# Group statistics, maxima and bias of a linear-attention block: fp32 matmuls of TensorE moved to VectorE or to one-pass matmuls

## The chip, the cores and the metric

One core of one Trainium2 chip. The metric is the device time of one execution of the program in microseconds; 1215.1 us is the median of three runs of the kernel before (1214.41 to 1216.41).

## The reference

x is 16 images of 64x64 positions with 256 channels, float32. Cut to what is computed:

```
g = group_norm(x)                       # 32 groups of 8 channels, over all positions
q, k, v = split(g @ W_qkv)              # 4096 positions x 256 each
k = softmax(k over the 4096 positions)  # per channel
context = k^T @ v                       # 256 x 256
y = x + (q @ context) @ W_out + b_out
```

The normalization is a scale and a shift per channel, so it can be folded into the matrices: the keys come from x times (scaled W_k), and q, context, W_out, the scale and the skip connection fold into one matrix M per image, so that y = x @ M + bias. The bias of an image is b_out plus what the shift by the mean contributes.

## The kernel before, in words

An image is cut into 8 chunks of 512 positions, a chunk into 4 tiles of 128. x is loaded in two layouts: xt (channels on the partitions, for keys and output) and x_raw (positions on the partitions, for the gather). fp32 precision comes from splitting every operand into a high part (type fp32r, which TensorE takes in one pass) and a low part (the rest), and from adding three one-pass products: high x high, high x low, low x high. ScalarE makes most high parts (xt_hi L676, x_hi L681, e_hi L693), GpSimd the low parts of x (xt_lo L341, x_lo L347), VectorE those of the exponentials (e_lo L924). A matmul whose operands are plain fp32 stands in the trace as two instructions.

Per image b there are three stages on TensorE, interleaved with those of the neighbours:

1. Keys (L399): for each chunk 24 matmuls into ps_k, two chunks in flight. ScalarE copies them to e_raw (L685); VectorE keeps a running maximum mx over the positions (L892). The softmax works with two blocks of 4 chunks (HALF = 4), each with its own maximum per channel.
2. After a block's 4 chunks: turn_max (L447) transposes mx by two TensorE transposes, VectorE reduces along the free axis (block_max, L901), spread_max (L455) brings the maximum back as a row on all 128 partitions by fp32 matmuls against the identity, into PSUM, and VectorE's shift subtracts it from e_raw (L917). ScalarE then takes the exponentials.
3. Gather (L480 to L492): exponentials times x, 24 matmuls a chunk, block 0 into ps_g0, block 1 into ps_e. alpha scales the two blocks to one maximum (block_scales, L906 and L909, then ScalarE's scales, L703). Then combine_u and combine_m make M; take_m ends them on VectorE (L982 to L993).
4. Output (L564, L573): per chunk of 512 positions two halves h of 128 output channels, six matmuls of 512 columns each, into ps_e. ScalarE adds the bias on its way to o_stage (L733), SP stores. The halves wait for o_ready of the same half one chunk earlier.

The chunks of the output are issued in the order 3, 4, 5, 6, 7, 0, 1, 2, with the keys of the next image between them. Block 0's turn_max and spread_max of the next image stand around its chunk 4; block 1's stand inside the gather.

The statistics of image b+1: VectorE's bn_half and bn_sum make per-channel mean and variance; stats_mean and stats_var (L462, L466) average them over groups of 8 channels by an fp32 matmul with the matrix grp; mean_of and var_of finish them on VectorE, rstd_of on GpSimd (L357). bias_sum (L542) multiplies the full-precision M with the negative mean: four fp32 matmuls with one moving column each, placed inside the first output chunk; bias_of (L1001) adds b_mean.

The order of the work on each engine is written out by hand: `images` calls `period` for each image on each engine, and each engine works through its list in order, with semaphore waits. GpSimd in `period`: xt_low(n,0), rstd_of(n), x_low(b,4..7), xt_low(n,1), xt_low(n,2), x_low(n,0..3), xt_low(n,3..7), where n = b+1. SP issues every DMA in order too: the loads of xt for the next image wait for e_ps, the stores for o_ready, the loads of xs (for the statistics of image b+2) for bn_done. The last three output halves of image 14 are kept back and issued in the last image's stages (`late`).

Of the kernel before, what the change touches and what calls it, by code (L numbers as in the profile page):

```python
# [28 lines left out]
POOL_LOW = 3  # L29


def build(nc: bass.Bass, xt: bass.AP, xn: bass.AP, w: bass.AP, b_out: bass.AP, out: bass.AP):
# [11 lines left out]
    with ExitStack() as ctx:  # L44
# [43 lines left out]
        b_col = sb("b_col", [P, CB])  # L88
# [5 lines left out]
        grp = sb("grp", [P, P])  # L94
# [31 lines left out]
        b_mean = sb("b_mean", [P, CB])  # L126
# [18 lines left out]
        filled = sem("filled")  # L145
        consts_ready = sem("consts_ready")
# [88 lines left out]
        def _(sp):  # L235
# [83 lines left out]
        def _(pool):  # L319
            nc.gpsimd.memset(one_col[:], 1.0).then_inc(consts_ready, 1)  # L320
# [51 lines left out]
            def period(b, parity, more, more2):  # L372
                n, np_ = b + 1, 1 - parity
                if more:
                    xt_low(n, np_, 0)
                    if b:
                        rstd_of(n, np_)
# [4 lines left out]
                if more:  # L382
# [7 lines left out]
                    for j in range(3, NCH):  # L390
                        xt_low(n, np_, j)
# [5 lines left out]
        def _(pe):  # L397
# [44 lines left out]
            def turn_max(b, blk):  # L442

                to = max_psum(b, blk)
                pe.wait_ge(max_done, b * (TILES * NCH) + TILES * HALF * (blk + 1))
                for d in range(CB):
                    last = nc.tensor.transpose(to[:, 0, d * P:(d + 1) * P], mx[:, d * P:(d + 1) * P], ident)  # L447
                last.then_inc(t_ps, 1)

            def spread_max(b, blk):  # L450

                to = max_psum(b, blk)
                pe.wait_ge(m_blk_ready, b * 2 + (blk + 1))
                for d in range(CB):
                    last = nc.tensor.matmul(to[:, 1, d * P:(d + 1) * P],  # L455
                                            m_blk[:, blk, d:d + 1].broadcast_to([P, P]), ident,
                                            start=(d == 0), stop=True, skip_group_check=True)
                last.then_inc(bc_ps, 1)

            def stats_mean(b):  # L460
                pe.wait_ge(mv_ready, b + 1)
                nc.tensor.matmul(stats_psum(b, 0), grp[:], mv[:, :, 0], start=True, stop=True).then_inc(mean_ps, 1)  # L462

            def stats_var(b):
                pe.wait_ge(var2_ready, b + 1)
                nc.tensor.matmul(stats_psum(b, 1), grp[:], var2[:], start=True, stop=True).then_inc(var_ps, 1)  # L466
# [71 lines left out]
            def bias_sum(b, parity):  # L538
                pe.wait_ge(m_full_ready, b + 1)
# [298 lines left out]
        def _(dve):  # L838
# [312 lines left out]
```

## Time and profile before

| | us |
|---|---|
| median of 3 runs | 1215.1 |
| profiled execution | 1214.93 |
| its span | 1213.2 |
| TensorE busy | 1190.1 |
| VectorE busy | 842.1 |
| ScalarE busy | 840.1 |
| GpSimd busy | 622.4 |

Granted TensorE clock: 1.00 of full speed over the span (2.4 GHz), in every one of the 40 slices. DMA moves 266.71 MB, 220 GB/s in the mean. Times in the profile are microseconds from the span's start. A busy time counts overlapping instructions of an engine once.

### The profile page before, as it was taken

The page shows a single profiled execution, that of the slowest core. Times are in us where ns is not written, and L with a number is a line of the kernel's source. Part 1 is how long each engine was busy: PE and PEld are TensorE (multiplying, and loading weights), DVE is VectorE, ACT ScalarE, POOL GpSimd, SP SyncE. Part 2 cuts the span into 40 slices and gives each one's busy share as a digit, 9 for nine tenths or more (in the row PEclk, how much of TensorE's full clock was granted, in tenths as well). Part 3 has the DMA queues.
Part 4 walks back from the last instruction along what each step waited for, and adds up shares of the span by engine and source line. Part 5 has one row for each costly group of instructions (what it writes and reads, how often), then busy time and mean ns, then how long its engine had stood idle before and what let it go on. Part 6 is the DMA issues. An engine that isn't in the chain of part 4 may idle for free.

```text
span 1213.2 us, 21447 instructions
## 1 busy us (share of the span) xinstructions
PE 1190.1 (98%) x8460; PEld 1115.8 (92%) x8460; DVE 842.1 (69%) x1582; ACT 840.1 (69%) x1140; POOL 622.4 (51%) x288
## 2 busy tenths in 40 slices
PE   4999999999999999999999999999999999999998
PEld 4998999999899998999989999899999989999897
DVE  6877667676776767768776677766767676676551
ACT  5767768677685776757677686776857768577664
POOL 8664564635645355563655636356463564536520
PEclk9999999999999999999999999999999999999999
DMA  9448666576765758666486665867657576573524
GB/s 339 146 167 294 218 235 205 195 269 208 274 203 199 264 172 294 226 206 237 162 301 229 221 227 183 286 209 252 204 201 263 193 278 225 201 252 122 191 74 170
DMA packets 107077, 266.71 MB, mean 220 GB/s; under 512 B 10208, under 2 KB 10208, under 8 KB 106976
## 3 DMA queue, kind: packets, MB, share of 16 engines
q1 hardware_dynamic: 106976, 265.33, 63.5%
q8 instruction: 67, 1.10, 0.4%
q14 instruction: 34, 0.28, 0.1%
HBM read 198.18 MB, written 67.11 MB: 219 GB/s over the span
## 4 chain that ended last, share of the span: by engine, by line
PE 93%; DVE 2%; ACT 1%; POOL 1%; DMA 1%; issue 1%; SPq 0%; DVEq 0%; POOLq 0%; ACTq 0%
PE ps_k L399 29%; PE ps_e L564 19%; PE ps_e L573 10%; PE ps_g L492 5%; PE ps_e L480 5%; PE ps_e L492 5%; PE ps_e L482 5%; PE ps_g L480 4%; PE ps_g L482 4%; PE ps_g L511 1%; PE ps_g L528 1%; PE ps_g L542 1%; PE ps_g L534 1%; POOL x_lo L347 1%; DVE mx L892 1%
## 5 line engine op out<-in xcount | busy, mean ns | idle before, releaser
L341 POOL TENSOR_TENSOR xt_lo<-xt_raw,xt_hi 128x1024 fp32r<-128x1024 f32 x128 | 307.4, 2404 | 434.5 <-ACT xt_hi L676 309.1
L347 POOL TENSOR_TENSOR x_lo<-x_raw,x_hi 128x1024 fp32r<-128x1024 f32 x128 | 281.4, 2216 | 65.6 <-ACT x_hi L681 56.2
L892 DVE TENSOR_TENSOR mx<-ps_k,mx 128x256 f32<-128x256 f32 x480 | 203.3, 424 | 95.8 <-ACT e_raw L685 74.3
L733 ACT ACTIVATE o_stage<-ps_e,bias 128x512 f32<-128x512 f32 x253 | 170.9, 689 | 114.1 <-PE ps_e L573 114.1
L399 PE MATMUL ps_k<-wk_hi,xt_hi 128*128 128x256 f32 x1024 | 207.1, 284 | 1.0 <-DVE mx L892 0.7
L399 PE MATMUL ps_k<-wk_lo,xt_hi 128*128 128x256 f32 x1024 | 205.5, 283 | 0.0
L685 ACT ACTIVATE e_raw<-ps_k 128x512 f32<-128x512 f32 x256 | 141.4, 596 | 87.2 <-PE ps_k L399 87.2
L849 DVE BATCH_NORM_STATS2 bn<-xs 128x6 f32<-128x512 f32 x240 | 154.5, 686 | 40.7 <-DMA xs<-in_xt_dram 39.5
L693 ACT ACTIVATE e_hi<-e_raw 128x1024 fp32r<-128x1024 f32 x128 | 135.1, 1055 | 60.9 <-DVE e_raw L917 33.0
L399 PEld LDWEIGHTS ps_k<-wk_hi,xt_hi 128*128 128x128 f32 x1024 | 163.4, 190 | 8.7 <-issue 1.8
L399 PE MATMUL ps_k<-wk_hi,xt_lo 128*128 128x256 f32 x1024 | 158.2, 283 | 0.0
L399 PEld LDWEIGHTS ps_k<-wk_lo,xt_hi 128*128 128x128 f32 x1024 | 157.4, 189 | 0.0
L564 PE MATMUL ps_e<-xt_hi,acc_hi 128*128 128x512 f32 x474 | 150.3, 398 | 0.0
L573 PE MATMUL ps_e<-xt_hi,u_lo 128*128 128x512 f32 x474 | 150.2, 398 | 0.0
L564 PE MATMUL ps_e<-xt_lo,acc_hi 128*128 128x512 f32 x474 | 148.8, 395 | 0.0
L681 ACT ACTIVATE x_hi<-x_raw 128x1024 fp32r<-128x1024 f32 x128 | 134.5, 1050 | 11.4 <-DMA x_raw<-in_xn_dram 11.2
L676 ACT ACTIVATE xt_hi<-xt_raw 128x1024 fp32r<-128x1024 f32 x128 | 135.0, 1055 | 3.8 <-DMA xt_raw<-in_xt_dram 3.8
L399 PEld LDWEIGHTS ps_k<-wk_hi,xt_lo 128*128 128x128 f32 x1024 | 137.3, 189 | 0.0
L480 PE MATMUL ps_e<-x_hi,e_hi 128*128 128x258 f32 x512 | 125.8, 283 | 0.7 <-POOL x_lo L347 0.7
L482 PE MATMUL ps_e<-x_lo,e_hi 128*128 128x256 f32 x512 | 125.5, 282 | 0.0
L482 PE MATMUL ps_g<-x_lo,e_hi 128*128 128x256 f32 x512 | 124.8, 281 | 0.0
L480 PE MATMUL ps_g<-x_hi,e_hi 128*128 128x258 f32 x512 | 124.8, 282 | 0.0
(129 smaller groups left out, 1992.7 us busy)
## 6 DMA issues: line engine op xcount, KB each, us to landing
xt_raw<-in_xt_dram SPq DMA_DIRECT2D x128, 512.0 KB, 4.3
x_raw<-in_xn_dram SPq DMA_DIRECT2D x128, 512.0 KB, 3.5
out_dram<-o_stage SPq DMA_DIRECT2D x127, 512.0 KB, 4.5
xs<-in_xt_dram SPq DMA_DIRECT2D x240, 256.0 KB, 5.1
w_setup<-in_w_dram SPq DMA_DIRECT2D x2, 256.0 KB, 10.1
out_dram<-o_stage SPq DMA_DIRECT2D x2, 256.0 KB, 2.0
wk<-in_w_dram SPq DMA_DIRECT2D x1, 256.0 KB, 9.9
wq_t<-in_w_dram SPq DMA_DIRECT2D x1, 256.0 KB, 10.9
```

The lines of the kernel that those rows point to most:

```text
L341: nc.gpsimd.tensor_tensor(xt_lo[:, s], xt_raw[:, s], xt_hi[:, s].bitcast(F32), ALU.subtract).then_inc(xt_lo_ready, 1)
L347: nc.gpsimd.tensor_tensor(x_lo[:, s], x_raw[:, s], x_hi[:, s, :, 0:C].bitcast(F32), ALU.subtract).then_inc(x_lo_ready, 1)
L399: return nc.tensor.matmul(ps_k[:, j % 2, t // 2, (t % 2) * C:(t % 2 + 1) * C], (xt_hi, xt_lo)[xs_][:, slot(j, parity), c, t * P:(t + 1) * ...
L480: nc.tensor.matmul(ps_g[j // HALF][:, d, 0:C + 2], w_, x_hi[:, j % X_SLOTS, t, :], start=(j % HALF == 0 and t == 0), stop=False, skip_grou ...
L482: nc.tensor.matmul(ps_g[j // HALF][:, d, 0:C], w_, x_lo[:, j % X_SLOTS, t, :], start=False, stop=False, skip_group_check=True)
L564: nc.tensor.matmul(out_psum(b, u, h), hi[:, c, h * P:(h + 1) * P], x_[:, s, c, :], start=(n == 0 and c == 0), stop=False, skip_group_check ...
L573: last = nc.tensor.matmul(out_psum(b, u, h), lo[:, c, h * P:(h + 1) * P], xt_hi[:, s, c, :], start=False, stop=(c == CB - 1), skip_group_c ...
L685: nc.scalar.activation(e_raw[:, j, 2 * h:2 * h + 2, :].rearrange("p t c -> p (t c)"), ps_k[:, j % 2, h, :], ACT.Copy).then_inc(k_out, 1)
L693: nc.scalar.activation(e_hi[:, j % E_SLOTS], e_raw[:, j], ACT.Exp).then_inc(e_hi_ready, 1)
L733: nc.scalar.activation(o_stage[:, u % O_SLOTS, h, :], src, ACT.Identity, bias=bias[:, h:h + 1]).then_inc(o_ready, 1)
L849: nc.vector.bn_stats(bn[:, q % CB, q // CB, :], xs[:, q % S_SLOTS, :]).then_inc(bn_done, 1)
L892: nc.vector.tensor_tensor(mx[:], tile, mx[:], ALU.max).then_inc(max_done, 1)
```

## The change

Four things are changed.

- Maxima: turn_max is gone. block_max on VectorE transposes mx in 32x32 squares, reduces each square's rows (quad), moves the results of the partition quarters 1 to 3 to quarter 0 (`move`, a reduce over one element) and reduces again. m_blk, m_all, dm and alpha_q are now 32 partitions by 8. block_diag splits the maxima into high and low part on partitions 0 to 31 and 32 to 63 and multiplies them with stacked 32x32 identities into diag (in u_hi's second half). spread_max is one fp32r matmul of 256 columns: a one-column weight of ones, spread to 128, times diag. spread_scales moves alpha_q back to 128 partitions in 4 moves.
- Statistics: for images 1 to 15 the inputs of the group sums are split into high and low parts (mean_parts, var_parts) and summed in one fp32r matmul of 4 columns; VectorE adds the two results.
- Bias: bias_sum is gone. VectorE multiplies u's product in ps_g0, which take_m reads too, with mean times rstd (scale_mean, b_terms), transposes, reduces, moves, adds b_out and moves back to two columns.
- Output: the second chunk goes to ps_g0, and its halves wait for b_terms_ready; the third waits for the outputs of the first. The first chunk is issued high(h0), high(h1), low(h0), low(h1).

GpSimd gets waits: on var_parts_ready (images after the first) and diag_ready ahead of xt_low(n, 0), and on diag_ready of block 0 ahead of xt_low(n, 5). ScalarE makes grp_r, one_r and eyes at the start. In the first image, block 1's spread_max stands one chunk later in the gather. b_out is loaded as 32x8.

The core of the diff:

```diff
-            def turn_max(b, blk):
-                to = max_psum(b, blk)
-                pe.wait_ge(max_done, b * (TILES * NCH) + TILES * HALF * (blk + 1))
-                for d in range(CB):
-                    last = nc.tensor.transpose(to[:, 0, d * P:(d + 1) * P], mx[:, d * P:(d + 1) * P], ident)
-                last.then_inc(t_ps, 1)
             def spread_max(b, blk):
-                pe.wait_ge(m_blk_ready, b * 2 + (blk + 1))
-                for d in range(CB):
-                    last = nc.tensor.matmul(to[:, 1, d * P:(d + 1) * P],
-                                            m_blk[:, blk, d:d + 1].broadcast_to([P, P]), ident, ...)
+                pe.wait_ge(diag_ready, b * 2 + (blk + 1))
+                nc.tensor.matmul(max_psum(b, blk)[:, 1, 0:C], one_r[:].broadcast_to([P, P]), diag,
+                                 start=True, stop=True).then_inc(bc_ps, 1)
...
+            return (ps_g0 if u == 1 else ps_e)[:, h, :]          # out_psum
...
-                elif u > 0:
-                    pe.wait_ge(o_ready, b * (CB * NCH) + (CB * (u - 1) + h + 1))
+                elif u > 1:
+                    pe.wait_ge(o_ready, b * (CB * NCH) + (CB * (u - 2 if u == 2 else u - 1) + h + 1))
+                elif u == 1:
+                    pe.wait_ge(b_terms_ready, b + 1)
...
                 emit_high(b, parity, 0, 0)
-                bias_sum(b, parity)
+                emit_high(b, parity, 0, 1)
                 emit_low(b, parity, 0, 0)
-                emit_high(b, parity, 0, 1)
                 emit_low(b, parity, 0, 1)
...
             def block_max(b, blk):
+                nc.vector.transpose(turned[:], mx[:]).then_inc(turned_ready, 1)
+                nc.vector.tensor_reduce(quad[:, :, 0], turned[:].rearrange("p (q k) -> p q k", k=Q), AX_X, ...)
+                for r in range(1, QUADS):
+                    last = move(quad[0:Q, :, r], quad[r * Q:(r + 1) * Q, :, 0])
+                nc.vector.tensor_reduce(m_blk[:, blk, :], quad[0:Q], AX_X, ALU.max).then_inc(m_blk_ready, 1)
+            def block_diag(b, blk):
+                move(m_parts[0:Q, :], m_blk[:, blk, :]).then_inc(m_part_hi_ready, 1)
+                nc.vector.tensor_tensor(m_parts[Q:2 * Q, :], m_blk[:, blk, :], m_parts[0:Q, :].bitcast(F32), ...)
+                nc.vector.tensor_tensor(diag..., eyes[:]..., m_parts[:]..., ALU.mult).then_inc(diag_ready, 1)
...
             def bias_of(b):
+                nc.vector.tensor_scalar(b_terms[:, 0, :], ps_g0[:, 0, 0:C], scaled_mean[:, 0:1], None, ALU.mult)
+                nc.vector.scalar_tensor_tensor(out=b_terms[:, 0, :], in0=ps_g0[:, 1, 0:C],
+                                               scalar=scaled_mean[:, 1:2], in1=b_terms[:, 0, :], ...)
+                nc.vector.transpose(b_terms[:, 1, :], b_terms[:, 0, :])
+                nc.vector.tensor_reduce(b_quad[:, 0, :], ...)
+                for r in range(1, QUADS):
+                    last = move(b_quad[0:Q, r, :], b_quad[r * Q:(r + 1) * Q, 0, :])
+                nc.vector.tensor_reduce(b_all[:], ...)
+                for r in range(QUADS):
+                    last = move(bias[r * Q:(r + 1) * Q, :], by_quad[:, :, r])
...
             def period(b, parity, more, more2):              # GpSimd
+                if more and b:
+                    pool.wait_ge(var_parts_ready, n)
+                pool.wait_ge(diag_ready, b * 2 + 2)
                 if more:
                     xt_low(n, np_, 0)
```

VectorE's order: block_max is followed by block_diag everywhere; after block 1's pair come mean_of, block_scales and shift(4), and spread_scales stands ahead of take_first; scale_mean stands ahead of take_u.

## Rows read from the trace of the kernel before

**Rows 1.** Busy us of each engine, its share of the span, its instructions (page).
```profile
PE 1190.1 (98%) x8460; PEld 1115.8 (92%) x8460; DVE 842.1 (69%) x1582; ACT 840.1 (69%) x1140; POOL 622.4 (51%) x288
```
**Rows 2.** Waits of TensorE: who waits for whom, total us, times, longest us.
```profile
PE ps_k L462 <- DVE mv L855: 15.3, 1, 15.3
PE ps_k L447 <- DVE mx L892: 1.9, 2, 1.6
...
PE ps_e L480 <- POOL x_lo L347: 0.7, 2, 0.4
```
**Rows 3.** TensorE's timeline around bias_sum (start, us, what), and that line's instructions.
```profile
675.07 0.95 PE L542 MATMUL ps_g<-neg_mean,acc 128*128 128x1 f32 x8
...
676.43 0.63 PE L564 MATMUL ps_e<-xt_hi,acc_hi 128*128 128x512 f32 x2
676.90 0.63 PE L564 MATMUL ps_e<-xt_lo,acc_hi 128*128 128x512 f32 x2
...
L542 PE MATMUL ps_g<-neg_mean,acc x128: 164/250/250, 82.9 to 1188.2; 128*128 128x1 f32 x128
```
**Rows 4.** TensorE's timeline around block 0's turn_max and spread_max.
```profile
618.06 0.38 PE L447 MATMUL ps_g<-zero_eye,mx 128*128 128x128 f32 x2
...
618.74 0.40 PE L399 MATMUL ps_k<-wk_hi,xt_hi 128*128 128x256 f32 x2
...
621.12 0.61 PE L455 MATMUL ps_g<-zero_eye,m_blk 128*128 128x128 f32 x4
...
622.03 0.63 PE L564 MATMUL ps_e<-xt_lo,acc_hi 128*128 128x512 f32 x2
```
**Rows 5.** TensorE's timeline in the gather stage.
```profile
643.32 0.38 PE L447 MATMUL ps_k<-zero_eye,mx 128*128 128x128 f32 x2
...
644.72 0.28 PE L480 MATMUL ps_g<-x_hi,e_hi 128*128 128x258 f32 x1
...
646.62 0.60 PE L455 MATMUL ps_k<-zero_eye,m_blk 128*128 128x128 f32 x4
...
648.25 0.28 PE L480 MATMUL ps_g<-x_hi,e_hi 128*128 128x258 f32 x1
...
650.15 1.12 PE L492 MATMUL ps_g<-x_hi,e_lo 128*128 128x258 f32 x8
651.11 0.28 PE L480 MATMUL ps_g<-x_hi,e_hi 128*128 128x258 f32 x1
...
653.98 0.28 PE L480 MATMUL ps_e<-x_hi,e_hi 128*128 128x258 f32 x1
```
**Rows 6.** VectorE's timeline: the running maximum of chunk 3.
```profile
615.60 1.87 DVE L892 TENSOR_TENSOR mx<-ps_k,mx 128x256 f32<-128x256 f32 x4 [2.66 <-ACT e_raw L685]
```
**Rows 7.** VectorE's timeline in the gather stage and at take_m's end.
```profile
640.81 1.22 DVE L924 TENSOR_TENSOR e_lo<-e_raw,e_hi 128x1024 fp32r<-128x1024 f32 x1
...
644.71 0.14 DVE L906 TENSOR_REDUCE m_all<-m_blk 128x2 f32<-128x4 f32 x1
644.89 0.83 DVE L909 TENSOR_TENSOR dm<-m_blk,m_all 128x4 f32<-128x4 f32 x1
...
647.26 1.22 DVE L917 TENSOR_TENSOR e_raw<-e_raw,ps_k 128x1024 f32<-128x1024 f32 x1 [1.47 <-PE ps_k L455]
...
674.44 0.80 DVE L993 TENSOR_TENSOR u_lo<-acc,acc_hi 128x512 fp32r<-128x512 f32 x1
```
**Rows 8.** GpSimd's timeline: low parts, numbers as before.
```profile
617.08 2.40 POOL L341 TENSOR_TENSOR xt_lo<-xt_raw,xt_hi 128x1024 fp32r<-128x1024 f32 x1 [3.20 <-ACT xt_hi L676]
...
643.32 2.39 POOL L341 TENSOR_TENSOR xt_lo<-xt_raw,xt_hi 128x1024 fp32r<-128x1024 f32 x1 [7.96 <-ACT xt_hi L676]
...
650.20 2.20 POOL L347 TENSOR_TENSOR x_lo<-x_raw,x_hi 128x1024 fp32r<-128x1024 f32 x1
...
685.42 2.39 POOL L341 TENSOR_TENSOR xt_lo<-xt_raw,xt_hi 128x1024 fp32r<-128x1024 f32 x1 [1.41 <-ACT xt_hi L676]
```
**Rows 9.** TensorE's timeline: low-part keys of chunk 3.
```profile
688.22 1.13 PE L399 MATMUL ps_k<-wk_hi,xt_lo 128*128 128x256 f32 x8
```

More of the change, by code:

```diff
@@ L29 @@
 POOL_LOW = 3
+Q = 32
+QUADS = P // Q
 def build(nc: bass.Bass, xt: bass.AP, xn: bass.AP, w: bass.AP, b_out: bass.AP, out: bass.AP):
@@ L93, in build @@
         eye = [zero_eye[:, P:3 * P], zero_eye[:, 0:2 * P]]
-        grp = sb("grp", [P, P])
+        with nc.sbuf_tensor("grp", [P, P], F32) as grp:
+            pass
+        grp_r = sb("grp_r", [P, P], F32R)
+        one_r = sb("one_r", [P, 1], F32R)
+        var_sum = sb("var_sum", [P, CB])
+        var_parts = sb("var_parts", [P, 2, CB], F32R)
+        mean_parts = sb("mean_parts", [P, 2, CB], F32R)
+        mean_rest = sb("mean_rest", [P, CB])
         mx = sb("mx", [P, C])
@@ L107, in build @@
         u_lo = sb("u_lo", [P, CB, C], F32R)
+        with nc.sbuf_tensor("turned", [P, C], F32) as turned:
+            pass
+        with nc.sbuf_tensor("b_terms", [P, CB, C], F32) as b_terms:
+            pass
         u_hi = sb("u_hi", [P, CB, C], F32R)
+        diag = u_hi[:, 1, :]
         m_lo = u_lo
@@ new lines, in stats_mean @@
+            def stats_mean(b):
+                if b == 0:
+                    pe.wait_ge(mv_ready, 1)
+                    nc.tensor.matmul(stats_psum(b, 0), grp_r[:].bitcast(F32), mv[:, :, 0], start=True,
+                                     stop=True).then_inc(mean_ps, 1)
+                else:
+                    pe.wait_ge(max_done, b * (TILES * NCH))
+                    pe.wait_ge(mean_parts_ready, b)
+                    nc.tensor.matmul(stats_psum(b, 0), grp_r[:], mean_parts[:].rearrange("p k c -> p (k c)"), start=True,
+                                     stop=True).then_inc(mean_ps, 1)
@@ new lines, in stats_var @@
+            def stats_var(b):
+                if b == 0:
+                    pe.wait_ge(var2_ready, 1)
+                    nc.tensor.matmul(stats_psum(b, 1), grp_r[:].bitcast(F32), var2[:], start=True,
+                                     stop=True).then_inc(var_ps, 1)
+                else:
+                    pe.wait_ge(var_parts_ready, b)
+                    nc.tensor.matmul(stats_psum(b, 1), grp_r[:], var_parts[:].rearrange("p k c -> p (k c)"), start=True,
+                                     stop=True).then_inc(var_ps, 1)
@@ L536, in combine_m @@
                     last.then_inc(m_ps, 1)
-            def bias_sum(b, parity):
-                pe.wait_ge(m_full_ready, b + 1)
-                for h in range(CB):
-                    for c in range(CB):
-                        last = nc.tensor.matmul(ps_g0[:, 0, h:h + 1], m_full[:, c, h * P:(h + 1) * P],
-                                                neg_mean[:, parity, c:c + 1], start=(h == 0 and c == 0),
-                                                stop=(c == CB - 1), skip_group_check=True)
-                last.then_inc(bias_ps, 1)
-            def out_psum(b, u, h):
-                if late(b, u, h):
-                    return (ps_k[:, 1, 0, :], ps_k[:, 1, 1, :], ps_k[:, 0, 0, :])[LATE.index((u, h))]
-                return ps_e[:, h, :]
             def emit_high(b, parity, u, h):
@@ L619, in period @@
                 gather_high(b, 0)
-                turn_max(b, 1)
                 if more and b:
@@ L627, in period @@
                     stats_var(n)
-                gather_low(b, 1)
-                for j in range(2, NCH):
+                gather_low(b, 2 if b == 0 else 1)
+                for j in range(3 if b == 0 else 2, NCH):
                     gather(b, j)
```

208 lines of the change are left out of this document (159 added, 49 removed).

## The prediction

> **What bounds the kernel now.** I read the busy shares first, then the waits of each engine, then the timeline of one image from the middle (about 612 to 690 us), because an average can't say which wait ends last. TensorE is busy for 1190.1 of 1213.2 us, VectorE for 842.1 [rows 1]. Of the 23 us that TensorE isn't busy, 15.3 stand before its first matmul; after that its waits are short: 1.9 us for VectorE's running maximum, 0.7 us for GpSimd's low parts of x [rows 2]. So TensorE's own stream is the bound: a microsecond taken out of it is a microsecond of the kernel, as long as nobody else becomes late. The cost of a matmul is not its "mean ns", since matmuls overlap, but the distance between starts: 0.47 us for two of 512 columns (676.43 to 676.90) [rows 3], 0.96 us for eight of about 256 (650.15 to 651.11), so 0.12 each [rows 5].
>
> **What leaves TensorE's stream.** Each price is the distance over the odd instructions, less the ordinary pace of those between.
> - bias_sum: 675.07 to 676.43 is 1.36 us with one ordinary pair of 0.47 [rows 3]: 0.89 us for its eight instructions (an fp32 matmul stands as two; 128 of them, 16 images, by the row that counts them there). 16 x 0.89 = 14.2 us.
> - turn_max: 618.06 to 618.74 is 0.68 us and holds four ordinary matmuls of 256 columns, 0.48 [rows 4]: 0.20 us, twice per image, 32 times, 6.4 us.
> - spread_max as it was: 621.12 to 622.03 is 0.91 us with one pair of 0.47 [rows 4]: 0.44 us, 32 times, 14.1 us.
> - The statistics' matmuls, each in front of eight low-part matmuls of 0.96 us: 643.32 to 644.72 is 1.40, so turn and mean cost 0.44 and the mean 0.24; 646.62 to 648.25 is 1.63, so spread and variance cost 0.67 and the variance 0.23 [rows 5]. 15 images: 7.0 us.
> Together 41.7 us.
>
> **What comes in.** One spread of 256 columns in the one-pass type per block. No row has it in its place; ordinary matmuls of that width and type pace at 0.12 us [rows 5], and half the old spread would be 0.22. I take 0.14, near the ordinary one: 32 x 0.14 = 4.5 us. Each statistic becomes one matmul of four columns for two instructions of two: not dearer than half the old pair, 0.11, and not below nothing; I take 0.10 of it, since the old price for next to no columns must be weights: 3.0 us. Net 34.2 us (with the bounds, 31 to 38). The order high, high, low, low of the first output chunk issues the same twelve matmuls: nothing. With turn_max its wait of 1.9 us goes [rows 2]; 1.6 of it is one wait in the first image, where GpSimd's low parts were late as well (two waits, 0.7) [rows 2], so of that wait and of the first image's own 1.0 us of matmuls I expect 0.5 back. 34.2 - 1.0 + 0.5 is 34 us.
>
> **What VectorE takes over, and when.** Chained operations of 128x256 take 0.45 us each (four in 1.87) [rows 6]; a tiny one of 0.14 us is followed after 0.18 (644.71 to 644.89) [rows 7]. No row has a transpose or a move between quarters of the partitions. I take the transpose as an ordinary 128x256 operation (bounds 0.3, and 1.2 as the 1024-element row at 640.81), a move as 0.2 (bounds 0.07 and 0.45). A block's chain is transpose, reduce, three moves, reduce, move, subtract, multiply: 3 x 0.45 + 7 x 0.2 = 2.8 us (1.9 to 5.2). Twice per image that is 5.6 us less two old reduces of the same width, 0.9; the bias adds 0.47 x 2 + 0.45 x 2 + 9 x 0.2 = 3.6; statistics and scales some 2. VectorE rises by 10 us per image, 160 in all, to some 1000 of 1185 us: no bound by its sum. What counts is where the pieces stand.
> - Block 1, in the gather: VectorE ends its low part at 642.0 [rows 7], the chain ends at 644.8. TensorE wants it at 646.62 less 0.3 gained before: 1.5 us of slack. GpSimd is held by the new wait and doesn't disturb.
> - Block 0, in the output stage: the maxima of chunk 3 end at 617.5 [rows 6]; the spread stands at 621.12 [rows 4], 0.2 earlier without the turn. 3.4 us for a chain of 2.8: slack 0.6. GpSimd's xt_lo of chunk 4 runs there until 619.5 [rows 8]; the chain's first operation with two SBUF inputs comes at 619.7.
> - Bias: take_m ends at 675.2 [rows 7]. The two multiplications end at 676.2, and TensorE wants b_terms_ready ahead of the second output chunk: 12 large and 24 small matmuls after 674.1, so 679.8. The bias itself is there at 678.8 instead of 676.2, and ScalarE's first two output chunks start 2 us late. That is what the gather's banks pay for: chunk 1 goes there and waits for no o_ready. Queued behind on ScalarE are keys_out of chunk 2 and later xt_hi of chunk 3, ready at 685.3, whence GpSimd's xt_lo of chunk 3, 685.42 to 687.81, wanted at 688.22 [rows 8, 9]: slack 0.4. ScalarE's work between (two outputs, two keys_out, two outputs) is 3.5 us within 6.5, so I cost it at nothing; a bias more than 1.5 us later than I say costs what it exceeds. On SP the store of chunk 0 goes out 1 us later, and the xs and xt loads behind it.
>
> **A stall that I expect.** dm in block_scales (two SBUF inputs, four elements) took 0.83 us where a tiny operation takes 0.15: from 644.89 to 645.72, just when GpSimd's xt_lo (643.32, 2.39 us) ends [rows 7, 8]. The change lets GpSimd start that xt_lo at var_parts_ready, 644.8 + 1.2 = 646.0, one step ahead of dm. So dm ends at 648.5, and shift(4), which stood at 647.26 and could stand at 646.8, comes right behind it. The variance, rstd on GpSimd and x_lo of chunk 4 follow. That x_lo ended at 652.40 and was wanted at 653.98 [rows 5, 8], slack 1.58. The chain gets 1.3 us later and TensorE reaches that point 0.75 us sooner (0.44 - 0.10 and 0.67 - 0.24): 0.5 us of stall in 14 images, 7 us (bounds 0 and 1.2 each, 17 us).
> The Trainium skill, "SBUF — State Buffer", section "SBUF: two separate sides", says that the port pair GpSimd shares with VectorE is an exclusive lock against VectorE instructions with two SBUF inputs: the first to start keeps it for the whole instruction. By that rule, the trace agrees: dm ends with the xt_lo. By a mere sharing of bandwidth dm would cost 0.3 us and the stall would be none, which is rival (a).
> The Trainium skill, "VectorE: DVE Perf Modes", section "Two Vector instructions with no wait between them", holds an instruction back until all earlier ones are finished if its input starts in another quarter of the partitions than the last one read. By it the three moves don't overlap; without it each chain would be some 0.3 us shorter. No row here shows such a move.
>
> **Sum.** The profiled execution took 1214.9 us around its span of 1213.2; the median shown is 1215.1, so one and the same. 1214.9 - 34 + 7 = 1188.
>
> **Rivals.**
> (a) No stall: dm gets in front of GpSimd, or they merely share. 1214.9 - 34 = 1181; for it: all slacks in the rows are positive.
> (b) New waits eat a good part: block 0's chain is nearer 4.5 us than 2.8, or the late bias reaches xt_lo of chunk 3. About 1 us more per image, 15 in all, over (a) or half over the forecast: 1196 to 1200. For it: slacks of 0.4 and 0.6 us. Against: VectorE idles ahead of both points.
> (c) Slower than before: block 0's spread decides. Its chain is one string of dependent operations with 3.4 us for it, and each microsecond beyond is paid by TensorE in full in every image. The gain per image is 2.2 us, so it loses from a chain of 5.6 us on: all its upper bounds (5.2) and GpSimd's lock caught once, up to 2.4 us. At 6 us that is 1214.9 - 34 + 15 x 2.6, about 1220. Against: the lock ends at 619.5, before it matters.
> (d) The change doesn't do what it says: the fp32 instructions leave, but the new matmuls, with one column of weights spread over 128 and four moving columns, cost what the old ones did. Then bias_sum and turn_max alone pay: 1214.9 - 14.2 - 6.4 + 5 of the stall, 1199.
>
> **Chances.** The forecast (1184 to 1192) 0.40, (a) 0.28, (b) 0.17, (d) 0.06, (c) 0.04, between or beyond 0.05. The range that leaves two in ten out is 1177 to 1200. What this measurement can't tell from no change is 0.2% of 1215, 2.4 us. Faster 0.93, same 0.03, slower 0.04.
>
> **What would show it.** Right: no TensorE instruction of turn_max or bias_sum; a spread with a variance in front of eight low-part matmuls adds 0.24 us to their 0.96; dm near 2.4 us; TensorE waits some 7 us in all for x_lo; the distance from image to image falls from 73.7 us (82.9 to 1188.2 in 15 steps, [rows 3]) to 72.0. Wrong: waits of TensorE ahead of a spread or of the second output chunk; waits for xt_lo of chunks 3 and 4; a spread over 0.2 us; over 73 us from image to image.

## The result: slower, and the profile after

| | before | after |
|---|---|---|
| median, us | 1215.6 (1214.4 to 1216.4, 5 runs) | 1222.5 (1219.9 to 1224.9, 5 runs) |
| ratio | | 1.0055 [1.0044, 1.0066] |
| profiled execution, its span, us | 1214.9, 1213.2 | 1219.9, 1218.2 |
| granted TensorE clock | 1.000 | 0.997 |

The forecast was 1188. The busy line of the page after answers to [rows 1]; below it is the chain of work that ended last.

```profile
PE 1168.8 (96%) x8142; PEld 1083.9 (89%) x8142; DVE 994.5 (82%) x2168; ACT 837.8 (69%) x1146; POOL 620.9 (51%) x289
...
PE 39%; DVE 28%; DMA 16%; ACT 6%; POOL 5%; issue 5%; SPq 0%; DVEq 0%; POOLq 0%; ACTq 0%
```

TensorE works 21 us less and 318 matmuls fewer in a longer span. VectorE is busy for 994.5 us (foretold: some 1000). The waits of TensorE (who for whom, total, times, longest), as in [rows 2]:

```profile
PE ps_e L615 <- ACT o_stage L781: 14.1, 15, 1.7
PE ps_e L543 <- POOL x_lo L404: 4.6, 15, 0.3
PE ps_k L461 <- POOL xt_lo L398: 3.4, 12, 0.3
PE ps_g L555 <- DVE e_lo L1047: 2.7, 1, 2.7
```

L615 is emit_high (before: L564), L543 the gather's high part (L480), L461 the keys (L399). In the first row TensorE can't write an output chunk into its half of PSUM, because ScalarE hasn't copied the chunk before out of it to o_stage. By the distances between starts these waits cost a little more than their rows say: o_stage 15.4 us, x_lo 6.5, xt_lo 5.7. From gather start to gather start a middle image took 74.0 us before and takes 74.0 (means of 13 steps); the first takes 82.2 instead of 76.5. So two questions: what eats the 2.2 us that TensorE saves in every image, and what costs the first one 5.7.

**The matmuls went as priced.** TensorE's timeline in the gather (start, duration), against [rows 5]:

```profile
649.24 0.28 PE L545 MATMUL ps_g<-x_lo,e_hi 128*128 128x256 f32 x1
649.36 0.17 PE L518 MATMUL ps_k<-mean_parts,grp_r 128*128 128x4 f32 x1
649.39 1.21 PE L555 MATMUL ps_g<-x_hi,e_lo 128*128 128x258 f32 x8
650.44 0.28 PE L543 MATMUL ps_g<-x_hi,e_hi 128*128 128x258 f32 x1
...
652.35 0.28 PE L507 MATMUL ps_k<-u_hi,one_r 128*128 128x256 f32 x1
652.47 0.17 PE L528 MATMUL ps_k<-var_parts,grp_r 128*128 128x4 f32 x1
652.50 1.21 PE L555 MATMUL ps_g<-x_hi,e_lo 128*128 128x258 f32 x8
653.54 0.28 PE L543 MATMUL ps_g<-x_hi,e_hi 128*128 128x258 f32 x1
```

Spread, variance and eight low-part matmuls take 653.54 - 652.35 = 1.19 us, 0.23 over their 0.96 (foretold 0.24); the mean adds 0.12 (foretold 0.10). The spread paces at 0.12 (taken: 0.14).

**VectorE's chain and dm went as priced too.** VectorE's timeline around block 1's maxima, then GpSimd's:

```profile
648.02 0.44 DVE L991 STREAM_TRANSPOSE turned<-mx 128x256 f32<-128x256 f32 x1
648.49 0.42 DVE L993 TENSOR_REDUCE quad<-turned 128x8 f32<-128x256 f32 x1
648.95 0.50 DVE L896 TENSOR_REDUCE quad<-quad 32x8 f32<-32x8 f32 x3
...
650.06 0.43 DVE L1014 TENSOR_TENSOR u_hi<-eyes,m_parts 128x256 fp32r<-128x256 f32 x1
...
651.93 2.41 DVE L1024 TENSOR_TENSOR dm<-m_blk,m_all 32x16 f32<-32x16 f32 x1
```
```profile
651.90 2.41 POOL L398 TENSOR_TENSOR xt_lo<-xt_raw,xt_hi 128x1024 fp32r<-128x1024 f32 x1 [9.76 <-DVE var_parts L946]
```

The chain ends at 650.49 (650.06 and 0.43) after 2.5 us (foretold 2.8). GpSimd's xt_lo starts 0.03 us ahead of dm, and dm ends with it, 0.83 before and 2.41 now; TensorE then waits 15 times for x_lo. That is the stall foretold as 7 us (measured 6.5).

**Where the gain goes.** VectorE's timeline from the end of take_m to the first shift of the next image:

```profile
680.17 0.79 DVE L1114 TENSOR_TENSOR u_lo<-acc,acc_hi 128x512 fp32r<-128x512 f32 x1
680.88 0.47 DVE L1121 TENSOR_SCALAR b_terms<-ps_g,scaled_mean 128x256 f32<-128x256 f32 x1
...
683.67 0.62 DVE L896 TENSOR_REDUCE bias<-b_all 32x2 f32<-32x2 f32 x4
684.33 1.87 DVE L980 TENSOR_TENSOR mx<-ps_k,mx 128x256 f32<-128x256 f32 x4
...
694.11 0.69 DVE L908 BATCH_NORM_STATS2 bn<-xs 128x6 f32<-128x512 f32 x1 [1.51 <-DMA xs<-in_xt_dram]
...
696.96 0.45 DVE L991 STREAM_TRANSPOSE turned<-mx 128x256 f32<-128x256 f32 x1
...
701.38 1.95 DVE L908 BATCH_NORM_STATS2 bn<-xs 128x6 f32<-128x512 f32 x3 [0.75 <-DMA xs<-in_xt_dram]
703.25 1.20 DVE L1040 TENSOR_TENSOR e_raw<-e_raw,ps_g 128x1024 f32<-128x1024 f32 x1
```

ScalarE behind it, and TensorE behind that:

```profile
704.49 1.06 ACT L744 ACTIVATE e_hi<-e_raw 128x1024 fp32r<-128x1024 f32 x1 [3.69 <-DVE e_raw L1040]
705.45 1.04 ACT L750 ACTIVATE e_raw<-e_raw 128x1024 f32<-128x1024 f32 x1
706.39 1.25 ACT L781 ACTIVATE o_stage<-ps_e,bias 128x512 f32<-128x512 f32 x2
```
```profile
704.81 1.10 PE L461 MATMUL ps_k<-wk_hi,xt_lo 128*128 128x256 f32 x8
707.12 0.74 PE L615 MATMUL ps_e<-xt_hi,acc_hi 128*128 128x512 f32 x2 [1.20 <-ACT o_stage L781]
```

ScalarE sits idle for 3.69 us, and output chunk 4, whose last matmuls end at 703.08, lies in PSUM until 706.39, because the exponentials of chunk 0, which wait for VectorE's shift, stand in its list ahead of the two copies. TensorE could start chunk 5 at 705.76 (704.81 and eight matmuls) and starts at 707.12: 1.36 us. The arithmetic closes against the trace of before. There take_m's last operation ends at 675.24 (674.44 and 0.80), shift(0) starts at 696.56, chunk 5 at 701.17: 21.3 and 25.9 us. Now take_m ends at 680.96 (680.17 and 0.79), and the shift comes 703.25 - 680.96 = 22.3 us after it, 1.0 later, and TensorE could be there after 24.8, 1.1 sooner. Before, the first copy of chunk 4 ended some 0.8 us ahead of chunk 5 (699.71 + 0.69 against 701.17). 1.0 + 1.1 - 0.8 = 1.3.

And VectorE no longer has room there. Its wait for keys (mx on e_raw) was 74.3 us in 47 times before and is 13.3 in 17.

### The profile page after: what moved, and what is told of

Its sections match the earlier page's. It is cut to its first block, busy times and chain, and to the rows that moved or that the text cites. A ratio compares the mean times of both kernels' runs of the same rounds, so it can differ in the third digit from the quotient of the medians.

```text
span 1218.2 us, 21452 instructions
## 1 busy us (share of the span) xinstructions
PE 1168.8 (96%) x8142; PEld 1083.9 (89%) x8142; DVE 994.5 (82%) x2168; ACT 837.8 (69%) x1146; POOL 620.9 (51%) x289
## 4 chain that ended last, share of the span: by engine, by line
PE 39%; DVE 28%; DMA 16%; ACT 6%; POOL 5%; issue 5%; SPq 0%; DVEq 0%; POOLq 0%; ACTq 0%
DMA xs<-in_xt_dram 15%; PE ps_k L461 10%; PE ps_e L615 7%; PE ps_e L543 5%; PE ps_e L555 5%; PE ps_e L545 5%; DVE mx L980 4%; DVE bn L908 4%; DVE e_raw L1040 3%; PE ps_e L624 3%; DVE dm L1024 3%; POOL x_lo L404 3%; ACT e_raw L750 2%; POOL rstd L414 2%; ACT o_stage L781 2%
## 5 line engine op out<-in xcount | busy, mean ns | idle before, releaser
L980 DVE TENSOR_TENSOR mx<-ps_k,mx 128x256 f32<-128x256 f32 x480 | 202.7, 422 | 35.3 <-ACT e_raw L736 13.3
L781 ACT ACTIVATE o_stage<-ps_e,bias 128x512 f32<-128x512 f32 x221 | 145.3, 688 | 101.9 <-PE ps_e L624 49.5
L461 PE MATMUL ps_k<-wk_hi,xt_hi 128*128 128x256 f32 x1024 | 206.6, 284 | 2.3 <-DVE mx L980 1.5
L461 PE MATMUL ps_k<-wk_lo,xt_hi 128*128 128x256 f32 x1024 | 204.6, 282 | 0.0
L908 DVE BATCH_NORM_STATS2 bn<-xs 128x6 f32<-128x512 f32 x240 | 155.4, 686 | 47.5 <-DMA xs<-in_xt_dram 46.4
L461 PEld LDWEIGHTS ps_k<-wk_hi,xt_hi 128*128 128x128 f32 x1024 | 163.4, 189 | 13.7 <-ACT xt_hi L727 3.6
L461 PE MATMUL ps_k<-wk_hi,xt_lo 128*128 128x256 f32 x1024 | 158.8, 283 | 3.5 <-POOL xt_lo L398 3.4
L461 PEld LDWEIGHTS ps_k<-wk_lo,xt_hi 128*128 128x128 f32 x1024 | 157.2, 188 | 0.0
L727 ACT ACTIVATE xt_hi<-xt_raw 128x1024 fp32r<-128x1024 f32 x128 | 135.2, 1057 | 15.5 <-DMA xt_raw<-in_xt_dram 15.4
L615 PE MATMUL ps_e<-xt_hi,acc_hi 128*128 128x512 f32 x414 | 131.8, 400 | 13.2 <-ACT o_stage L781 13.2
L461 PEld LDWEIGHTS ps_k<-wk_hi,xt_lo 128*128 128x128 f32 x1024 | 136.8, 188 | 6.4 <-POOL xt_lo L398 6.4
L543 PE MATMUL ps_e<-x_hi,e_hi 128*128 128x258 f32 x512 | 127.5, 287 | 4.6 <-POOL x_lo L404 4.6
L615 PE MATMUL ps_e<-xt_lo,acc_hi 128*128 128x512 f32 x414 | 130.3, 396 | 0.0
L624 PE MATMUL ps_e<-xt_hi,u_lo 128*128 128x512 f32 x414 | 127.7, 395 | 0.0
L543 PE MATMUL ps_g<-x_hi,e_hi 128*128 128x258 f32 x512 | 124.6, 281 | 0.0
```

Source lines behind the costliest of these rows:

```text
L461: return nc.tensor.matmul(ps_k[:, j % 2, t // 2, (t % 2) * C:(t % 2 + 1) * C], (xt_hi, xt_lo)[xs_][:, slot(j, parity), c, t * P:(t + 1) * ...
L543: nc.tensor.matmul(ps_g[j // HALF][:, d, 0:C + 2], w_, x_hi[:, j % X_SLOTS, t, :], start=(j % HALF == 0 and t == 0), stop=False, skip_grou ...
L615: nc.tensor.matmul(out_psum(b, u, h), hi[:, c, h * P:(h + 1) * P], x_[:, s, c, :], start=(n == 0 and c == 0), stop=False, skip_group_check ...
L624: last = nc.tensor.matmul(out_psum(b, u, h), lo[:, c, h * P:(h + 1) * P], xt_hi[:, s, c, :], start=False, stop=(c == CB - 1), skip_group_c ...
L727: nc.scalar.activation(xt_hi[:, s], xt_raw[:, s], ACT.Copy).then_inc(xt_hi_ready, 1)
L781: nc.scalar.activation(o_stage[:, u % O_SLOTS, h, :], out_psum(b, u, h), ACT.Identity, bias=bias[:, h:h + 1]).then_inc(o_ready, 1)
```

## The experiments

Each is measured against the kernel before on the same chip; that kernel had medians from 1214.3 to 1215.8. E4, E6 and E7 leave the bias out of the output. The summary:

| | median us | ratio, interval |
|---|---|---|
| E1 GpSimd waits for dm | 1211.2 | 0.9973 [0.9951, 0.9994] |
| E2 shift(0) sooner | 1247.6 | 1.0261 [1.0246, 1.0277] |
| E3 both | 1232.5 | 1.0140 [1.0125, 1.0155] |
| E4 no bias tail (nothing behind b_terms) | 1199.2 | 0.9869 [0.9852, 0.9885] |
| E5 E1 + three early statistics | 1204.5 | 0.9912 [0.9897, 0.9927] |
| E6 tail computed, not used | 1219.2 | 1.0026 [1.0014, 1.0039] |
| E7 E1 + E4 | 1189.9 | 0.9798 [0.9781, 0.9814] |
| E8 second chunk back in ps_e | 1223.3 | 1.0074 [1.0056, 1.0092] |
| E9 ScalarE's copies first | 1241.9 | 1.0208 [1.0189, 1.0228] |
| E10 E5 + E9 | 1220.8 | 1.0038 [1.0024, 1.0052] |
| E11 E10 + xt_lo held for e_lo | 1194.9 | 0.9838 [0.9823, 0.9853] |
| E12 E9 + xt_lo held for e_lo | 1216.7 | 1.0005 [0.9990, 1.0021] |

**E1, E2, E3.** E1 takes the lock off dm, E2 takes four statistics out of the way of shift(0), E3 does both.

```diff
# E1, GpSimd in period
-                pool.wait_ge(diag_ready, b * 2 + 2)
+                pool.wait_ge(dm_ready, b + 1)
# E2, VectorE in period
+                shift(n, 0)
                 bn_halves(8, 12)
-                shift(n, 0)
```

> The changed kernel with one edit: GpSimd waits for dm_ready (block_scales done) instead of diag_ready ahead of xt_low(n,0), so its xt_lo starts behind dm and no longer locks it out. Theory L (dm's lock costs what stands behind it): dm falls from 2.27 to about 0.16 us, the 0.47 us stall of TensorE on x_lo of chunk 4 goes in 14 images (6.5 us), and in the first image the 2.8 us wait on e_lo, the wait of 0.6 behind it and the half clock of 6.8 us (3.4 us) go too: 1222.5 - 6.5 - 6 = about 1210. Rival A (anchored elsewhere: the later wait of TensorE on ScalarE's o_stage ends last, and it grows by what is saved before it): images stay at 73.9 us, only the first image gains, about 1216. Rival F (VectorE is simply full): the order of work doesn't matter, 1222 less at most 2.

> The changed kernel with one edit: VectorE does shift(n,0) ahead of bn_halves(8,12) instead of behind, so the exponentials of chunk 0 and the output halves queued behind them on ScalarE don't wait for the xs loads. Theory X (the o_stage wait of 1.0 to 1.9 us per image comes from shift(0) behind the xs loads): the wait on o_stage falls from 14.1 us to under 2, time 1222.5 - 14 = about 1208; the stalls on x_lo of chunk 4 (0.47) and xt_lo (0.45) stay. Rival A' (the bn work only moves: chunk 4's maxima and the later exponentials are late instead): o_stage waits reappear one chunk later, 1219 or more. Rival F (VectorE full): no change, 1222.

> Both edits: GpSimd waits for dm_ready, and shift(n,0) ahead of bn_halves(8,12). If the two stalls are separate their gains add: 1222.5 - 12.5 - 14 = about 1196. If they are one chain (what one gives the other takes), it is no better than the better of the two alone, within 2 us. Rival F (VectorE full): over 1218.

E1's time came as expected. dm falls from a mean of 2.27 us to 0.16, the x_lo wait is gone, o_stage is untouched; TensorE's waits in E1:

```profile
PE ps_e L615 <- ACT o_stage L781: 14.1, 15, 1.7
PE ps_k L461 <- POOL xt_lo L398: 3.0, 11, 0.3
```

The lock didn't vanish, it moved to a cheaper place. The xt_lo that now starts behind dm (131.43, 2.40 us in the second image) still runs when the e_lo behind shift(4) starts, here in VectorE's timeline:

```profile
133.29 1.62 DVE L1047 TENSOR_TENSOR e_lo<-e_raw,e_hi 128x1024 fp32r<-128x1024 f32 x1
```

In 14 images this e_lo takes 1.62 to 1.69 us instead of 1.22, and TensorE waits for none of them.

E2 removed the o_stage wait (0.8 us left) and was 25 us slower than the changed kernel; E3 was 10 us slower. No expectation had such times. E2's VectorE and GpSimd timelines show what took its place:

```profile
721.66 2.52 DVE L1047 TENSOR_TENSOR e_lo<-e_raw,e_hi 128x1024 fp32r<-128x1024 f32 x1
...
728.20 2.37 DVE L1047 TENSOR_TENSOR e_lo<-e_raw,e_hi 128x1024 fp32r<-128x1024 f32 x1
```
```profile
720.69 2.41 POOL L398 TENSOR_TENSOR xt_lo<-xt_raw,xt_hi 128x1024 fp32r<-128x1024 f32 x1 [3.51 <-ACT xt_hi L727]
...
727.09 2.40 POOL L398 TENSOR_TENSOR xt_lo<-xt_raw,xt_hi 128x1024 fp32r<-128x1024 f32 x1 [3.98 <-ACT xt_hi L727]
```

e_lo of chunks 0 and 1, 1.22 us long in the changed kernel, now start inside GpSimd's xt_lo and last 2.4 and 2.5. VectorE reaches the gather late, and TensorE waits for var_parts (13.3 us), x_lo (11.1) and mx (6.4). E3 has the same fault without dm's. So the o_stage wait alone is not the price: removing it moved the phases of two engines onto each other. That this lock is what made E2 slow is read from its trace and was not tried on E2; E9 to E12 come back to it.

**E4, E6, E7: what the bias tail costs.** E4 and E7 replace everything behind b_terms by a memset:

```diff
-                nc.vector.transpose(b_terms[:, 1, :], b_terms[:, 0, :]).then_inc(b_turned_ready, 1)
...
-                    last = move(bias[r * Q:(r + 1) * Q, :], by_quad[:, :, r])
-                last.then_inc(bias_ready, 1)
+                nc.vector.memset(bias[:], 0.0).then_inc(bias_ready, 1)
# E6: the tail stays; ScalarE neither waits for it nor reads it
-                                     bias=bias[:, h:h + 1]).then_inc(o_ready, 1)
+                                     bias=no_bias[:, h:h + 1]).then_inc(o_ready, 1)
```

> The changed kernel with the bias left out after the two multiplications (transpose, reduces and moves gone, zero written instead, so the output lacks the bias): VectorE gets some 2.7 us less per image, and ScalarE's first output starts that much sooner. Theory B (the late bias delays output, store, xs and xt loads behind it): the wait of 0.45 us on xt_lo goes (6 us), and the xs loads come early enough that most of the o_stage wait goes too (10 of 14 us); dm's stall and the first image stay: about 1206. Rival: only the direct wait on bias matters, ScalarE idles 2.5 us there without TensorE waiting; gains under 3 us, 1220. Rival F (VectorE full: time falls in step with its work, 2.7 x 15 = 40 us): 1185 or less.

> The changed kernel, VectorE does all of bias_of, but ScalarE adds a constant zero column and waits for nothing of it (the output lacks the bias). It tells the two ways apart in which the bias tail costs 23 us (1222.5 against 1199.2 without the tail). If the lateness of ScalarE's output is what costs (output, store and loads behind it start 2.5 us late): about 1203, as without the tail. If VectorE's time is what costs (maxima, statistics, xs and shift(0) behind the tail): about 1220, as with it.

> Without the bias tail (the output lacks the bias) and with GpSimd waiting for dm_ready. If the lock's stall and the bias tail are separate, their gains add: 1199.2 - 12 = about 1187, nearly the blind sum without any stall (1181). If something else ends last by then: 1194 or more.

E4 gives back 23 us (expected 16), E6 only 3. In E4 the o_stage wait is 1.6 us and the one on xt_lo is gone. So what the tail costs is VectorE's time in a stretch where everything behind it is chained, not that ScalarE's output chunks get their bias 2 us late. E7 adds the dm edit: 1189.9, within 3 us of the 1187 expected, and its o_stage wait is 2.0 us in all. A middle image takes 71.9 us, 2.0 less than the 74.0 before, where the sum over TensorE's stream says 2.2. The whole kernel stays 9 us above that sum (1214.9 - 34 is 1181); 2.8 of them are the first step, 79.3 us instead of 76.5.

**E8: do the gather's banks matter?**

```diff
-            return (ps_g0 if u == 1 else ps_e)[:, h, :]
+            return ps_e[:, h, :]
...
-                elif u > 1:
-                    pe.wait_ge(o_ready, ...)
-                elif u == 1:
-                    pe.wait_ge(b_terms_ready, b + 1)
+                elif u > 0:
+                    pe.wait_ge(o_ready, b * (CB * NCH) + (CB * (u - 1) + h + 1))
```

> The changed kernel with the second output chunk back in ps_e, each half waiting for o_ready of the first chunk's same half. With the bias 2.5 us late ScalarE reads the first chunk's half 0 out at 685.0 in the image I looked at, and TensorE wants its bank at about 684.1: a wait of 0.9 us per image. Theory: if that wait adds, 1222.5 + 13 = 1235; if the images are anchored by VectorE's chain (73.9 us whatever TensorE does in between), the new wait only shortens the later one on o_stage: 1223 to 1226.

The o_stage wait grows to 18.8 us, 4.7 more and not the 13 expected, and the medians don't tell this from nothing (1.0074 against 1.0055, intervals overlapping). The time is that of the theory that VectorE's chain sets the image, but the trace doesn't bear it out. In the profiled execution (the slowest of the four, 1227.2 us) a middle image takes 74.3 us (12 steps; a thirteenth, 76.9, has a stretch of 3.4 us at half the clock) against 74.0, and that is about the 0.3 us that the wait grew. So the second chunk's bank is worth about 5 us at most, and whether a longer wait is won back elsewhere stays open.

**E5: less for VectorE in that stretch.**

```diff
+                bn_halves(0, 3)
                 take_second(b)
...
-                bn_halves(0, 4)
+                bn_halves(3, 4)
```
(and E1's line.)

> GpSimd waits for dm_ready as in the first experiment, and three of the four bn_halves(0,4) stand ahead of take_second, where VectorE idled 2.4 us per image, instead of behind the bias. Theory V (VectorE's stretch from the bias to chunk 4 of the output is one full chain, bias tail, maxima, statistics, in which the 2.9 us of bias tail come out as TensorE's waits on xt_lo and o_stage; lightening it by 2 us gives most of them back): waits on o_stage 14.1 to under 4 us, period 73.5 to about 72.5 us, time 1211 - 15 = about 1196. Rival D (the xs loads are bound by DMA bandwidth and not by when bn frees their slots): xs land when they did, VectorE waits for them instead, 1209 or more. Rival P (take_second gets late): TensorE waits in combine_u, about 1 us per image, 1220.

Three statistics move into the gather, where VectorE waits for TensorE anyway. 6.6 us better than E1, less than expected: 12.0 us of o_stage waits stay, and VectorE's waits for xs grow from 46.4 us in the changed kernel to 57.8. So a part of the rival, loads that land no earlier, isn't excluded. Of the versions that compute the bias it was the first ahead of the kernel before by a clear margin.

**E9 to E12: ScalarE's order, and the lock behind it.** E9 swaps two entries of ScalarE's list in the changed kernel; E10 does so in E5; E11 adds one wait to E10, E12 the same wait to E9.

```diff
# E9, E10, ScalarE in period
+                emit(b, 4)
                 if more:
                     exps(n, 0)
-                emit(b, 4)
# E11, E12, GpSimd in period
+                        if j > HALF + 1:
+                            pool.wait_ge(e_lo_ready, e_lo_count(n, j - HALF - 2))
                         xt_low(n, np_, j)
```

> The changed kernel with one swap on ScalarE: the two copies of output chunk 4 to o_stage stand ahead of the exponentials of chunk 0 of the next image, which wait for VectorE's first shift. Theory Q (the wait of TensorE on o_stage is only a queueing of ScalarE behind VectorE's lateness): the wait falls from 14.1 to under 3 us. If that wait were all that the image loses, 1222.5 - 11 = 1211. Theory V (the image is anchored by VectorE's chain, which this swap leaves as it is, as undoing the banks left the time as it was): the wait moves to another place of TensorE, to low parts or maxima that VectorE and GpSimd have ready no earlier, and the time stays within 1219 to 1223.

> The fastest whole kernel so far (GpSimd's xt_lo waits for dm, three of the next statistics stand in the gather) with the same swap on ScalarE. There 12 us of o_stage waits are left. Theory Q: they go, and 1204.5 - 9 = 1195. Theory V: VectorE's chain sets the image, the waits turn up elsewhere, 1202 to 1205.

Neither theory had these times: 19 and 16 us slower than without the swap. The o_stage wait went (0.8 us left in both), and the waits inside the gather came. E10's TensorE waits, then VectorE's and GpSimd's timelines (e_lo of chunk 1 is stretched so in 14 images):

```profile
PE ps_k L528 <- DVE var_parts L946: 13.5, 15, 1.0
PE ps_k L518 <- DVE mx L980: 5.8, 13, 0.8
PE ps_k L507 <- DVE u_hi L1014: 4.8, 15, 1.0
```
```profile
716.68 3.46 DVE L1047 TENSOR_TENSOR e_lo<-e_raw,e_hi 128x1024 fp32r<-128x1024 f32 x1
```
```profile
716.66 2.40 POOL L398 TENSOR_TENSOR xt_lo<-xt_raw,xt_hi 128x1024 fp32r<-128x1024 f32 x1 [1.71 <-ACT xt_hi L727]
```

xt_lo of chunk 7 starts 0.02 us ahead of e_lo of chunk 1, which waits it out: xt_lo ends at 719.06, e_lo 1.1 us later, at 720.14. In the changed kernel the same two stand at 713.64 and 712.50, e_lo first. The stall on o_stage had kept them apart. E11 puts the order down by a wait:

> The kernel of the run before (dm first, three early statistics, ScalarE's output copies of chunk 4 ahead of the exponentials) with GpSimd's xt_lo of chunks 6 and 7 held until VectorE has ended e_lo of chunks 0 and 1 of the same image. There e_lo of chunk 1 started at 716.68 us, 0.02 us after GpSimd's xt_lo of chunk 7, and took 3.46 us instead of 1.22; 15 of the 61 e_lo of that form account for 121.1 us of busy time instead of 80. Theory K (that lock is what made the swap on ScalarE slower, 2.2 us of VectorE per image): all e_lo are back at 1.22 us, the waits ahead of the variance, the means and the spread inside the gather (13.5, 5.8 and 4.8 us) fall to under 6 together, the o_stage wait stays gone, and the time is 1220.8 - 15 x 1.7 = 1195, below the 1204.5 of the kernel without the swap. Rival V (VectorE's sum of work anchors the image at about 73 us whatever stands where): 1203 to 1206. Rival W: the held xt_lo are late for TensorE's low keys of chunks 6 and 7 (wanted at 715.00 and 720.78, expected at 715.1 and 720.3): waits on xt_lo of over 0.5 us per image, 1205 or more.

1194.9, as expected. The waits in the gather are gone but for 1.0 us ahead of one spread and 0.2 ahead of one variance; the held xt_lo costs 1.4 us (4.4 for 3.0). E11's TensorE waits and its VectorE:

```profile
PE ps_k L463 <- POOL xt_lo L398: 4.4, 9, 0.8
...
PE ps_e L617 <- ACT o_stage L783: 0.8, 1, 0.8
PE ps_e L545 <- POOL x_lo L404: 0.7, 2, 0.4
```
```profile
697.00 1.21 DVE L1049 TENSOR_TENSOR e_lo<-e_raw,e_hi 128x1024 fp32r<-128x1024 f32 x1
```

The e_lo of chunks 0 and 1 are back at 1.2 us. Not all are: one in the gather of 14 images takes 1.7 to 2.3 us, as in E1 behind the xt_lo that waits for dm. A middle image takes 72.3 us (mean of 13). This version computes the bias too. It beats the kernel before by 1.6% [1.5%, 1.8%] and the changed one by some 2%. The added wait without the swap was not tried on E5; there no e_lo of chunks 0 and 1 is stretched.

> The changed kernel with only two edits: ScalarE's output copies of chunk 4 ahead of the exponentials, and GpSimd's xt_lo of chunks 6 and 7 held until VectorE's e_lo of chunks 0 and 1 are done. dm stays locked behind xt_lo. Theory Q with the lock (the o_stage wait costs about 1 us per image, and without the lock nothing takes its place): the o_stage wait under 2 us, x_lo's 4.6 us stay or grow a little, 1222.5 - 11 = 1211, between 1209 and 1214. Rival V (VectorE's sum of work anchors the image at about 74 us): 1218 or more, with waits for VectorE inside the gather.

E12 came 6 us too slow for its first theory and too fast for the rival. The o_stage wait fell to 0.8 as expected, but x_lo's rose from 4.6 to 9.8 and xt_lo's from 3.4 to 7.6:

```profile
PE ps_e L545 <- POOL x_lo L404: 9.8, 15, 0.8
PE ps_k L463 <- POOL xt_lo L398: 7.6, 17, 1.0
```

No e_lo is stretched in E12. But of the 13.3 us that TensorE no longer waits at the output chunks 9.4 come back in these two rows. 5.2 of them are x_lo's, which hangs on the locked dm (in E11, where dm is free, x_lo's row is 0.7); why xt_lo's grows isn't shown. The stalls stand in for each other in part, and so each edit by itself shows less than its share.

## Why the prediction was wrong

**TensorE's stream: right.** Net 34 us leave it. The spacings above agree within 0.02 us each. They come out as time only when the waits are gone: E7's middle image is 2.0 us shorter of the 2.2 foretold, and the kernel is 25 us faster than before.

**VectorE's durations: right.** A block's chain 2.5 us for 2.8, the bias 3.4 for 3.6, the sum 994.5 for 1000. The two sums counted one small operation too many: their lists have six and eight, not seven and nine, and give 2.55 and 3.44. Three moves don't overlap (0.50 us for three of 0.155), as the forecast took it; no run has moves that overlap, so its 0.3 us for the difference stays untested. Rivals (c), a long chain of block 0, and (d), dear new matmuls, are out: spreads wait once, 0.9 us in all. The forecast's reading that GpSimd's lock ends before it matters for block 0's chain was wrong, though it cost little. In 13 images xt_lo of chunk 4 holds the chain's first operation with two SBUF inputs for 0.2 to 0.3 us (0.38 to 0.50 instead of 0.16; the image shown above is an exception), 3.7 us of VectorE's time in all. One of them, inside an xt_lo from 622.07 to 624.45:

```profile
624.05 0.42 DVE L1009 TENSOR_TENSOR m_parts<-m_blk,m_parts 32x8 fp32r<-32x8 f32 x1
```

**dm behind GpSimd's xt_lo: right.** Duration, place and price; E1 isolates it, 11.3 us between the medians. Of the 9.9 between the profiled executions 7.0 lie in the middle images (73.5 us for 74.0) and 2.7 in the first step (79.5 for 82.2).

**The failed step: the late bias, of which I wrote "I cost it at nothing".** The prediction had three sentences on what VectorE's new work makes late: VectorE has "no bound by its sum"; ScalarE's work between is "3.5 us within 6.5"; on SP the loads go "1 us later". Each looked at one engine or at the two consumers nearest to the bias, chunk 1 and xt_lo of chunk 3. I followed the late bias into ScalarE's queue and not along VectorE's own: bias, maxima of chunks 1 to 3, eight statistics, each of which frees a buffer for a load, block 0's chain, four statistics, shift(0). For blocks 0 and 1 I took TensorE's earlier arrival off the slack; for xt_lo of chunk 3 I compared with its old 688.22, and for chunk 5 I compared nothing. But TensorE comes 1.1 us sooner there and VectorE 1.0 us later, and the slack at output chunk 5 was 0.8. No row group ahead of the prediction covers VectorE's and ScalarE's stretch up to that chunk. Measured, this costs 15.4 us of o_stage waits and 5.7 of waits for xt_lo, next below; with the tail left out (E4) both go to 1.6 us together and 23 us come back, though block 0's chain is still there. So the term put at nothing is the bias tail, and it cost 23.

The sign "waits for xt_lo of chunks 3 and 4" that I named as wrong appeared for chunk 4: xt_hi of chunk 4 waits for its load (0.50 us, at 695.32), xt_lo runs 696.47 to 698.87, and TensorE starts the low keys at 698.92. Over all images that is 5.7 us. SP issues that load (688.97, landed 695.30) in order behind four xs loads (686.82 to 688.60) that wait for VectorE's statistics; E5, which moves statistics ahead, has no such wait. That it is the order on SP was not tried by itself.

**The first image: missed.** I gave it half a microsecond to the good. VectorE's and GpSimd's timelines there:

```profile
53.76 1.43 DVE L1009 TENSOR_TENSOR m_parts<-m_blk,m_parts 32x8 fp32r<-32x8 f32 x1
...
55.75 2.41 DVE L1024 TENSOR_TENSOR dm<-m_blk,m_all 32x16 f32<-32x16 f32 x1
...
60.41 1.21 DVE L1047 TENSOR_TENSOR e_lo<-e_raw,e_hi 128x1024 fp32r<-128x1024 f32 x1
```
```profile
50.41 4.75 POOL L409 TENSOR_TENSOR e_lo<-e_raw,e_hi 128x1024 fp32r<-128x1024 f32 x2 [1.44 <-ACT e_raw L750]
55.72 2.41 POOL L398 TENSOR_TENSOR xt_lo<-xt_raw,xt_hi 128x1024 fp32r<-128x1024 f32 x1 [0.56 <-DVE u_hi L1014]
```

Two small VectorE operations are held, dm until 58.16, and e_lo of chunk 3 behind them ends at 61.62 (before: 58.10). TensorE waits 2.65 us for it, and then this follows (stretch, busy times, granted clock):

```profile
57.00:61.00 4.00, 2.02 (x17) 1.80 (x15) 4.00 (x5) 0.70 (x2) 3.28 (x2) 1.00 0.41 131
61.80:68.60 6.80, 6.45 (x29) 6.18 (x30) 6.37 (x22) 5.67 (x6) 2.58 (x2) 0.50 0.55 173
69.00:76.00 7.00, 6.37 (x52) 5.96 (x50) 5.35 (x8) 5.33 (x7) 4.29 (x3) 1.00 0.56 186
```

In the second stretch the granted clock is 0.50 (1.2 GHz of 2.4), and matmuls pace at 0.214 us instead of 0.12. The wait and the slow stretch, some 3 us each, make up the 5.7 us that the first step lost. Every profile of the changed kernel and its versions with dm locked has such a stretch of 6.8 us in the first image. Of those with the dm edit E1 and E11 have none, E3, E5, E7 and E10 one of 3.4 us.

**The sum again.** 1188, plus 15.4 (o_stage), 5.7 (xt_lo), 5.7 (first image) is 1215 of the profiled 1219.9. Of the remaining 5 us 1.1 stand ahead of one spread in the last image and 1.1 ahead of the keys' first matmuls in four images; the rest is open. Rival (b), new waits behind the late bias, had the right kind of mechanism, but two other places and 15 us at most. Rival (c) named 1220, which is nearly the time that came, but by a chain of 6 us that took 2.5: that its number fits is chance. The 0.04 for slower was too small because the gains on TensorE were not set against the losses on VectorE at the same point, output chunk 5.

## What to carry to other kernels

When work moves from a full engine to one with idle time, add up the receiver's work between two meetings with the full engine, and compare the slack left there with both shifts at once: the receiver's lateness and the giver's earliness. Then follow what the late engine releases (buffers, loads, the head of another engine's queue) to the end of the stage. When a stall is removed, look at which instructions of VectorE and GpSimd it kept apart, and write the good order down as a wait.

## What the runs showed of the hardware

- An instruction of VectorE with two SBUF inputs waits out a GpSimd tensor_tensor that started 0.02 to 0.03 us ahead, a small one and a large one alike: 16 elements per partition took 2.41 us instead of 0.16, 1024 elements 3.46 instead of 1.22. One that starts later is held until the GpSimd instruction ends (m_parts at 624.05). The Trainium skill, "SBUF — State Buffer", section "SBUF: two separate sides", gives this rule; the trace agrees. It holds the other way as well: GpSimd's xt_lo, started 0.25 us after an e_lo at 711.45, took 3.25 us instead of 2.40 (E10). What I had not expected is that a wait of 1 us on a third engine decides who is first.
- A 32x32-square transpose of 128x256 fp32 on VectorE takes 0.44 us, as an ordinary operation of that width. Three moves between quarters of the partitions take 0.50 us together, 0.17 from start to start, and four 0.62, 0.16 from start to start.
- A one-pass matmul of four columns with 128x128 weights adds 0.11 to 0.12 us between its neighbours, as much as one of 256.
